# Where a four-layer graph kernel adds up mask quarters, sums squares and takes its spare PSUM banks

## The chip, the cores and the metric

The program runs on one core of a Trainium2 chip. Its metric is the device time of one execution in microseconds (us). Three runs of the kernel before gave 1098.0, 1098.6 and 1100.78 us, so the median is 1098.6 us. The engines are called TensorE (PE in the profile), VectorE (DVE), ScalarE (ACT), GpSimd (POOL) and SyncE (SP).

## The reference

`x` has 8 batches of 2048 nodes with 64 channels. `adj` is a 2048 x 2048 matrix of edges, each row divided by its degree. Four layers follow, each of the form `x = layernorm(x + layer(x))`.

```python
# layer 0: Chebyshev terms of the matrix, weights of each node from its embedding
w = einsum('nd,dkio->nkio', embedding, weight); b = einsum('nd,do->no', embedding, bias)
x_g = [x, A @ x, 2 * A @ (A @ x) - x]
out = einsum('bnki,nkio->bno', x_g, w) + b
# layer 1: attention over entries of adj above 0.5, softmax, elu
# layer 2: ((adj + I) @ (x @ W.T + b)) / degree
# layer 3: v = x with node 0 replaced; three times:
effects = einsum('nm,bmd->bnd', adj, v)
h = relu(concat([v, effects]) @ W1.T + b1); v = h @ W2.T + b2
```

## The kernel before

Nodes lie on the partitions in 16 tiles; the 512 columns are batch times channel, cut into four chunks `c` of 128. A block `(c, j)` is four node tiles of one chunk, 128 partitions x 512 elements; there are 16. The mask (edges as 64 or 0, in fp8) stays in SBUF (`Bm`), and activations are split into a high and a low f16 half, so every product with the mask is two matmuls of 512 columns per tile.

The order of all work is written out by hand in lists that every engine's program walks, each engine picking the steps that it has a part in. `MIDDLE` (`middle_order`, from L94) is layer 0: for each of 64 tiles a step `Z` (36 matmuls against the weights, of which VectorE and ScalarE accumulate the results by the embedding), `add` on GpSimd, and `("bt", 4u + t)`; the norms of layer 0 and most of layer 1 are strewn among them. `TAIL` (`last_order`, from L147) holds layer 2 and the first product of layer 3 as steps `("P", k)`, k = 0 to 31, each a 512-column product over all 16 tiles, with an evacuation `("E", k)`; then the last two products of layer 3, in four halves n = 4 to 7. Each of those is made in Winograd's way by seven instead of eight quarter products: `("M", n, s, q)`, slots s = 0 to 6, for two columns of blocks each. Time there is counted in half slots h = 14 (n - 4) + 2 s + jj, 56 in all; `on(h, ...)` puts a step at the head of a half slot.

What the steps do:

- `bt` (L1581): one of 64 sums of quarters of the mask, 128x512 fp8 (T3, T2, T4, T1, 16 each, in this order; each waits for the one of the array before). The first matmul that needs them is `("M", 4, 2, 0)`, which waits for all 64 (`s_bt`).
- `V` (n, s, jj) (L1486): evacuation of a slot. In slots 1, 4, 5 and 6 a block is finished: `high` writes its high half, one more VectorE instruction the low half (`s_gl`). In slot 6 ScalarE's relu comes first.
- `G`: transform of a finished block by the weights into the input of the next product (PE by `by_weight`, L692; VectorE adds up). `cut` splits it into halves (ScalarE, then GpSimd). `mix`: Winograd's sums of the input, on VectorE.
- `gmax`, `gcol`, `step`: largest value of a half product, sent round the partitions through PE (L924), and a chain of ten small VectorE instructions that makes the next scales. `flags`, `total` (PE, L899), `verdict`: the test whether the input is of the kind that the fast path may take; `branch` stands before h = 28.
- `F` (c, j): last transform of a finished block, four instructions of VectorE add it to `X` (`s_y3`). Then the norm of that block: `sq` (ScalarE squares it into a buffer, VectorE sums groups of 64), `var3` (VectorE, then ScalarE's square root), `rs3` (five small VectorE instructions, L1429 to L1433) and `out` (VectorE multiplies, L1619; SyncE sends 256 KB). The steps F, sq and var3 stand together, rs3 and out one half slot later. 14 blocks go so before the last two (3, 0) and (3, 1).

PSUM has 8 banks. `take_banks` (L528) gives a slot of half product n a fixed pair of them: banks 2 and 3 for slots 1, 3, 5; banks 4 and 5 (n even) or 0 and 1 (n odd) for slots 0, 2, 4, 6. All other steps (`G`, `F`, `t22`, `gcol`, `total`) take turns in the list `banks`: 6, 7 and the two that this half product leaves free. Whoever takes a bank waits for the last reader of what was in it (`held`). Worked out from this, the first matmul of half product 7, `("M", 7, 0, 0)`, waits in bank 0 for `s_y3` = 7, the end of VectorE's part of `("F", 1, 0)`.

Of the kernel before, what the change touches and what calls it, by code (L numbers as in the profile page):

```python
# [93 lines left out]
def middle_order():  # L94
# [30 lines left out]
    for u in range(16):  # L125
# [21 lines left out]
def last_order(after):  # L147
# [34 lines left out]
    at(31, *mixes(4, 1, 1, 3, 2), cut(4, 1, "X12"), cut(4, 1, "S2"), *mixes(4, 1, 4))  # L182
    for k in range(32):
# [30 lines left out]
    on(15, ("total",))  # L214
    on(16, ("verdict",))
    between = {}
    for g in range(2):
        n, h = 6 + g, 14 * (2 + g)
        on(h + 1, ("fin", g))
        for s in ENDS:  # L220
            for jj in range(2):
                u, e = ending(n, s, jj), h + 2 * s + jj
                first, then = [("F", *u), ("sq", 3, *u), ("var3", *u)], [("rs3", *u), ("out", *u)]
                if e == 54:
                    between[55] = first
                    on(56, *then)
                elif e == 55:
                    on(56, *first, *then)
                else:
                    on(e + 2, *first)  # L230
                    on(e + 3, *then)
# [35 lines left out]
def gnn_kernel(nc, x_in, at_in, a_in, embt_in, sm_in, bx_in, w0_in, a12_in, w0bb_in, out):  # L267
    ctx = ExitStack()
    with ctx:
# [733 lines left out]
        def scalar_steps(e, steps):  # L1003
# [3 lines left out]
            for step in steps:  # L1007
# [28 lines left out]
                elif kind == "sq":  # L1036
# [6 lines left out]
                    if SQPREV[L, c, j] is not None:  # L1043
                        e.wait_ge(s_red, SQPREV[L, c, j] + 1)
                    fn(four(sq_buf(L, c, j)), xpart(c, j), ACT.Square).then_inc(s_sq, 1)
                elif kind in ("var", "var3"):
                    L, c, j = (*norm_key(step), 0)[:3]
                    e.wait_ge(s_var, VARN[norm_key(step)] + 1)
                    fn(st_part(L, c, j, 1), st_part(L, c, j, 2), ACT.Sqrt).then_inc(s_sd, 1)
# [255 lines left out]
        def vector_steps(e, steps, fc):  # L1305
# [44 lines left out]
            for step in steps:  # L1350
# [54 lines left out]
                elif kind == "sq":  # L1405
                    L, c, j = step[1:]
                    o = st_part(L, c, j, 0)
                    e.wait_ge(s_sq, SQN[L, c, j] + 1)
                    red(e, o if L == 3 else o[:, 8 * j:8 * j + 8], grid(sq_buf(L, c, j)), ALU.add).then_inc(s_red, 1)
                elif kind == "var":  # L1410
                    L, c = step[1:]
                    e.wait_ge(s_red, SQN[L, c, 3] + 1)
# [6 lines left out]
                elif kind == "var3":  # L1419
                    c, j = step[1:]  # L1420
                    u = order3(c, j)
                    e.wait_ge(s_red, SQN[3, c, j] + 1)
                    e.wait_ge(*((s_n[1], 16) if u < 2 else (s_n[3], u - 1)))
                    ts(e, st_part(3, c, j, 2), st_part(3, c, j, 0), 1 / 64, 1e-5 * 4096, ALU.mult, ALU.add).then_inc(s_var, 1)
                elif kind in ("rs", "rs3"):
                    L, c, j = (*norm_key(step), 0)[:3]
                    e.wait_ge(s_sd, VARN[norm_key(step)] + 1)
                    s0, s1, s2 = (st_part(L, c, j, k) for k in range(3))
# [41 lines left out]
                elif kind == "V" and step[2] not in (0, 2):  # L1470
# [17 lines left out]
                    e.wait_ge(s_gh, place(p, c, j) + 1)  # L1488
                    e.wait_ge(s_gl, place(p, c, j))
# [91 lines left out]
                elif kind == "bt":  # L1581

                    k, q = divmod(step[1], NT)
                    t, cols = q // 2, slice(512 * (q % 2), 512 * (q % 2) + 512)
                    quarters = {f"B{i}{j}": Bm[:, 8 * i - 8 + t, 1024 * j - 1024 + cols.start:1024 * j - 1024 + cols.stop]
                                for i in (1, 2) for j in (1, 2)}
                    d = {f"T{i}": BT[:, i - 1, t, cols] for i in (1, 2, 3, 4)}
                    e.wait_ge(s_bm, 2 * NT)
                    if k:
                        e.wait_ge(s_bt, NT * (k - 1) + q + 1)  # L1590
                    o, a, b, f = ((d["T3"], quarters["B22"], quarters["B12"], ALU.subtract),
                                  (d["T2"], d["T3"], quarters["B11"], ALU.add),
                                  (d["T4"], quarters["B21"], d["T2"], ALU.subtract),
                                  (d["T1"], quarters["B12"], quarters["B11"], ALU.subtract))[k]
                    e.tensor_tensor(o, a, b, f, saturate=False).then_inc(s_bt, 1)
# [600 lines left out]
```

## Time and profile before

| | |
|---|---|
| median of three runs | 1098.6 us |
| profiled execution, its own time | 1096.39 us |
| its span, first to last instruction | 1094.6 us |
| busy: PE, DVE, ACT, POOL | 1032.6, 781.2, 406.6, 456.2 us |
| mean granted TensorE clock | 0.986 |

The profile's rows tell start and length of an instruction in us, the engine, the line in the kernel (often a helper's: L1146 is every scalar_tensor_tensor, L1697 every sum on GpSimd), what it writes and reads, and in square brackets how long the engine had been idle and which instruction ended that. The names are those of the SBUF and PSUM tensors: `BW` is the mask and the sums of its quarters, `S` the split activations, `T` the finished blocks, `X` the running x, `WZ` the weights and later a scratch buffer.

### The profile page before, as it was taken

What the parts mean: (1) busy time and instruction counts of PE and PEld (TensorE: products, weight loads), DVE (VectorE), ACT (ScalarE), POOL (GpSimd) and SP (SyncE); (2) the same over time, 40 slices, a digit from 0 to 9 for tenths busy, and PEclk for the clock granted to TensorE, in tenths of its full rate; (3) what the DMA queues carried; (4) which work ended last, traced back from release to release, by engine and by line L of the source; (5) the groups of instructions that cost most, each with busy time, mean ns of one, the idle gap of its engine ahead of it and who ended that gap; (6) DMA issues with size and microseconds to landing.
All of it is one profiled execution on the core that took longest, in us unless ns stands there. A gap on an engine that the chain in (4) does not pass through costs nothing.

```text
span 1094.6 us, 18614 instructions
## 1 busy us (share of the span) xinstructions
PE 1032.6 (94%) x6922; PEld 494.2 (45%) x6922; DVE 781.2 (71%) x1887; ACT 406.6 (37%) x878; POOL 456.2 (42%) x543
## 2 busy tenths in 40 slices
PE   6989999999999999999999999999999999995993
PEld 2446444434443433334355555555545445552442
DVE  5855676778658876887776877785576867678556
ACT  3632233333334344444424644653445221221211
POOL 0003597546357766885662503443252322222000
PEclk9999999999999999999999999999999999998897
DMA  9750000000000000000010221112112000000111
GB/s 370 258 230 1 1 2 1 1 1 1 1 1 2 1 1 2 1 1 2 1 40 1 78 78 40 66 51 77 65 52 77 1 2 1 3 20 29 30 30 49
DMA packets 14657, 45.65 MB, mean 42 GB/s; under 512 B 960, under 2 KB 9280, under 8 KB 10080
## 3 DMA queue, kind: packets, MB, share of 16 engines
q1 hardware_dynamic: 14560, 44.39, 11.0%
q8 instruction: 57, 0.93, 0.3%
q14 instruction: 40, 0.33, 0.1%
HBM read 40.19 MB, written 4.19 MB: 41 GB/s over the span
## 4 chain that ended last, share of the span: by engine, by line
PE 73%; DVE 14%; POOL 3%; ACT 3%; issue 3%; DMA 2%; SPq 0%; DVEq 0%; ACTq 0%; POOLq 0%
PE PS L713 32%; PE PS L842 17%; PE PS L886 15%; DMA R<-at_in 2%; DVE X L1146 2%; DVE T L1146 2%; PE PS L699 1%; PE PS L700 1%; PE PS L698 1%; POOL X L1697 1%; ACT T L1005 1%; POOL T L1697 1%; DVE R L1146 1%; DVE T L1149 1%; DVE BW L1143 1%
## 5 line engine op out<-in xcount | busy, mean ns | idle before, releaser
L713 PE MATMUL PS<-BW,S 128*128 128x512 fp8e4 x1792 | 405.0, 380 | 8.1 <-DVE R L1146 4.0
L713 PEld LDWEIGHTS PS<-BW,S 128*128 128x128 f16 x1792 | 170.0, 98 | 216.1 <-issue 17.8
L842 PE MATMUL PS<-WZ,R 64*128 64x512 f16 x1536 | 198.9, 377 | 3.2 <-ACT T L1005 3.2
L1005 ACT ACTIVATE T<-PS,SM 128x128 f32<-128x128 f32 x384 | 112.8, 366 | 201.2 <-DVE X L1146 131.0
L1697 POOL TENSOR_TENSOR T<-T 128x128 f32<-128x128 f32 (+1 forms) x192 | 131.0, 682 | 120.5 <-ACT T L1005 109.6
L1146 DVE SCALAR_TENSOR_TENSOR X<-PS,SM,X 128x128 f32<-128x128 f32 x320 | 109.6, 342 | 28.2 <-PE PS L842 27.2
L886 PE MATMUL PS<-BW,S 128*128 128x512 fp8e4 x512 | 117.7, 384 | 10.8 <-DVE X L1146 10.3
L842 PEld LDWEIGHTS PS<-WZ,R 64*128 64x128 f16 x1536 | 69.0, 94 | 107.4 <-issue 25.4
L1697 POOL TENSOR_TENSOR S<-R,S 128x512 f16<-128x512 f32 x48 | 58.1, 1223 | 122.0 <-ACT S L1005 122.0
L842 PE MATMUL PS<-WZ,T 64*128 64x512 f16 x768 | 103.8, 376 | 0.0
L1697 POOL TENSOR_TENSOR T<-R,T 128x512 f16<-128x512 f32 x36 | 42.5, 1181 | 141.2 <-DVE T L1138 80.8
L1146 DVE SCALAR_TENSOR_TENSOR T<-PS,SM,T 128x128 f32<-128x128 f32 x256 | 87.8, 343 | 16.5 <-PE PS L842 16.2
L886 PEld LDWEIGHTS PS<-BW,S 128*128 128x128 f16 x512 | 49.4, 99 | 67.5 <-DVE X L1146 10.5
L1005 ACT ACTIVATE R<-PS,cs 128x512 f32<-128x512 f32 x48 | 32.7, 684 | 112.7 <-PE PS L707 79.0
L886 PE MATMUL PS<-BW,T 128*128 128x512 fp8e4 x320 | 72.8, 379 | 0.0
L698 PE MATMUL PS<-hat,T 128*128 128x128 f16 x320 | 57.2, 220 | 13.4 <-DVE T L1146 13.4
L1697 POOL TENSOR_TENSOR X<-X,T 128x128 f32<-128x128 f32 x128 | 62.6, 489 | 10.0
L765 PE MATMUL PS<-BW,S 128*128 128x512 fp8e4 x240 | 53.8, 386 | 9.3 <-DVE BW L1143 9.3
L842 PEld LDWEIGHTS PS<-WZ,T 64*128 64x128 f16 x768 | 37.4, 94 | 45.5
L700 PE MATMUL PS<-hat,T 128*128 128x128 f16 x320 | 57.2, 220 | 0.0
L699 PE MATMUL PS<-hat,T 128*128 128x128 f16 x320 | 57.2, 220 | 0.0
L1146 DVE SCALAR_TENSOR_TENSOR R<-PS,ra,R 128x128 f32<-128x128 f32 x192 | 52.6, 342 | 6.1 <-PE PS L700 3.5
(214 smaller groups left out, 1434.4 us busy)
## 6 DMA issues: line engine op xcount, KB each, us to landing
WZ<-a_in SPq DMA_DIRECT2D x16, 1024.0 KB, 4.8
R<-at_in SPq DMA_DIRECT2D x15, 1024.0 KB, 6.2
out<-X SPq DMA_DIRECT2D x16, 256.0 KB, 2.3
X<-x_in SPq DMA_DIRECT2D x3, 1024.0 KB, 14.3
T<-w_in SPq DMA_DIRECT2D x1, 1536.0 KB, 9.5
R<-at_in SPq DMA_DIRECT2D x2, 512.0 KB, 4.8
SM<-sm_in SPq DMA_DIRECT2D x1, 520.5 KB, 15.8
X<-x_in SPq DMA_DIRECT2D x2, 256.0 KB, 4.5
```

Of the source, the lines that this page charges most:

```text
L698: e.matmul(ok, th, hat[:, 0, kind, :], start=True, stop=False)
L699: e.matmul(ok, tl, hat[:, 0, kind, :], start=False, stop=False)
L700: m = e.matmul(ok, th, hat[:, 1, kind, :], start=False, stop=True)
L713: m = e.matmul(o, stile(h, t, c), Bm[:, t, block(j)], start=(t == 0 and h == 0), stop=(last and t == NT - 1 and h == 1))
L765: e.matmul(bank(2 * c + j), stile(h, jt, c), Bm[:, jt, block(j)], start=(jt == 0 and h == 0), stop=False)
L842: m = e.matmul(bank(b0 + q), halves[kd][zh][r, :], WZ[r, wh, kd, block(g)], start=(i == 0), stop=(i == 8))
L886: m = e.matmul(o, half_of(n, what, h, q % 2)[:, t, :], b[:, 4 * (q % 2) + t, :], start=(s in (0, 1, 3) and q % 2 == 0 and t == 0 and h == ...
L1005: return e.activation(o, i, f, **kw)
L1143: return e.tensor_scalar(o, i, 0.0, EDGE, ALU.not_equal, ALU.mult, saturate=False)
L1146: return e.scalar_tensor_tensor(out=o, in0=a, scalar=s, in1=b, op0=f, op1=g)
L1149: return e.tensor_reduce(o, i, op=f, axis=AX.X, apply_absolute_value=absolute, negate=negate)
L1697: return e.tensor_tensor(o, a, b, f)
```

## The change

It has these parts.

1. The 64 `bt` steps leave `MIDDLE` and VectorE; they stand in `TAIL` at k = 8 to 29, three to a k, and GpSimd makes them.
2. For n = 5, 6, 7 `gcol` and `step` stand one half slot later, `total` and `verdict` too.
3. From slot 4, second pair, to the end of a half product the other steps take turns in banks 6 and 7 alone.
4. The low half of the blocks of slot 6 is made by GpSimd for n < 7.
5. The norm of layer 3: for the first 14 blocks ScalarE sums the squares itself, in eight activations of 64 columns with an accumulator (`accum_out`) in place of one of 512 columns and VectorE's reduction. `var3` and `rs3` are made for two blocks at once (16 columns in place of 8), and stand later; the two last blocks keep their own. `out` of ten blocks (the first eight and (2, 2), (2, 3)) is made by GpSimd, of the other six by VectorE. `F` and `sq` of the 16 blocks are spread anew.

```diff
-            order += [("Z", u, t), ("add", u, t), ("bt", 4 * u + t)]
+            order += [("Z", u, t), ("add", u, t)]
...
+    for i in range(64):
+        at(8 + i // 3, ("bt", i))
...
-        on(h + 1, ("gcol", p, g), ("step", p, g))
-        on(h + 2, *take(n, 0, "X11"))
+        on(h + 2, ("gcol", p, g), ("step", p, g), *take(n, 0, "X11"))
...
-    on(15, ("total",))
-    on(16, ("verdict",))
+    on(16, ("total",))
+    on(17, ("verdict",))
     between = {}
+
+    for n, s, jj, h in ((6, 1, 0, 33), (6, 1, 1, 34), (6, 4, 0, 41), (6, 4, 1, 42), (6, 5, 0, 43), (6, 5, 1, 44), (6, 6, 0, 44),
+                        (6, 6, 1, 45), (7, 1, 0, 47), (7, 1, 1, 48), (7, 4, 0, 52), (7, 4, 1, 53), (7, 5, 0, 54), (7, 5, 1, 55)):
+        on(h, ("F", *ending(n, s, jj)), ("sq", 3, *ending(n, s, jj)))
+    for n, s, h in ((6, 1, 36), (6, 4, 43), (6, 5, 46), (6, 6, 47), (7, 1, 49), (7, 4, 54), (7, 5, 56)):
+        u = ending(n, s, 0)
+        on(h, ("var3", *u, 2), ("rs3", *u, 2), ("out", *u), ("out", *ending(n, s, 1)))
+    u, v = ending(7, 6, 0), ending(7, 6, 1)
+    between[55] = [("F", *u)]
+    w = half[56]
+    half[56] = [("sq", 3, *u), *w[:2], ("F", *v), ("sq", 3, *v), ("var3", *u, 1), ("rs3", *u, 1), *w[2:], ("out", *u),
+                ("var3", *v, 1), ("rs3", *v, 1), ("out", *v)]
...
+                        elif s == 4 and q == 2:
+                            banks = (6, 7)
...
+        def by_gpsimd(c, j):
+
+            return order3(c, j) < 8 or order3(c, j) in (12, 13)
+
+        def summed_by_act(c, j):
+
+            return order3(c, j) < 14
...
+                        o, q = four(sq_buf(L, c, j)), st_part(L, c, j, 0)
+                        for i in range(8):
+                            t, d = i // 2, slice(64 * (i % 2), 64 * (i % 2) + 64)
+                            m = fn(o[:, t, d], X[:, 4 * j + t, 128 * c + d.start:128 * c + d.stop], ACT.Square, accum_out=q[:, i:i + 1])
+                        m.then_inc(s_sq, 1)
...
+                    if s == 6 and n < 7:
+                        continue
                     e.wait_ge(s_gl, place(p, c, j))
                     stt(e, T[:, c, 1, block(j)], f, 0.0, T[:, c, 0, block(j)], ALU.max, ALU.subtract).then_inc(s_gl, 1)
```

In `gpsimd_steps` the code of `bt` is that of L1583 to L1595, word for word, and three kinds are new:

```diff
+                elif kind == "V" and step[1] < 7 and step[2] == 6:
...
+                    e.wait_ge(s_gh, k + 1)
+                    e.wait_ge(s_gl, k)
+                    add(T[:, c, 1, block(j)], RT[rt_buf(s, jj)], T[:, c, 0, block(j)], ALU.subtract).then_inc(s_gl, 1)
+                elif kind == "out" and by_gpsimd(*step[1:]):
+                    c, j = step[1:]
+                    e.wait_ge(s_rs, RSN[first_of(c, j)] + 1)
+                    e.wait_ge(s_n[3], order3(c, j))
+                    scaled(e, c, j).then_inc(s_n[3], 1)
```

By the same rules of `take_banks`, `("M", 7, 0, 0)` then waits for `s_cp` = 18, ScalarE's copy of `("t22", 6, 1)`, seven half slots earlier.

## Rows read from the trace of the kernel before

**Rows 1.** The page's part 4: the chain that ended last, by engine.
```profile
PE 73%; DVE 14%; POOL 3%; ACT 3%; issue 3%; DMA 2%; SPq 0%; DVEq 0%; ACTq 0%; POOLq 0%
```

**Rows 2.** Windows by stage: length, busy us (instructions) of each engine, clock, DMA share, GB/s.
```profile
113.00:546.00 433.00, 420.62 (x3170) 178.16 (x3172) 320.17 (x893) 166.98 (x478) 282.90 (x388) 1.00 0.00 1
546.00:812.00 266.00, 266.00 (x1776) 142.66 (x1773) 191.67 (x385) 125.59 (x188) 103.61 (x89) 1.00 0.15 56
812.00:990.00 178.00, 174.48 (x1069) 89.31 (x1067) 131.00 (x298) 52.03 (x81) 48.52 (x42) 1.00 0.05 17
990.00:1020.00 30.00, 14.52 (x75) 6.59 (x74) 22.33 (x58) 6.06 (x13) 4.50 (x3) 0.77 0.15 43
...
1072.00:1094.60 22.60, 5.25 (x38) 2.98 (x36) 14.78 (x48) 3.99 (x10) 0.00 (x0) 0.75 0.18 51
```

**Rows 3.** PE's timeline, 995 to 1020 us, and one undisturbed group of 16 at 1061.
```profile
995.18 0.22 PE L698 MATMUL PS<-hat,T 128*128 128x128 f16 x1 [1.78 <-DVE T L1146]
...
1003.49 0.22 PE L698 MATMUL PS<-hat,T 128*128 128x128 f16 x1 [3.38 <-DVE T L1146]
...
1014.64 5.58 PE L886 MATMUL PS<-BW,S 128*128 128x512 fp8e4 x16 [10.32 <-DVE X L1146]
...
1061.18 3.62 PE L886 MATMUL PS<-BW,S 128*128 128x512 fp8e4 x16
```

**Rows 4.** DVE's timeline, 1006 to 1014 us.
```profile
1006.47 1.12 DVE L1146 SCALAR_TENSOR_TENSOR X<-PS,R,X 128x128 f32<-128x128 f32 x4
1008.28 0.69 DVE L1149 TENSOR_REDUCE T<-WZ 128x8 f32<-128x512 f32 x1 [0.69 <-ACT WZ L1005]
...
1013.46 1.12 DVE L1146 SCALAR_TENSOR_TENSOR X<-PS,R,X 128x128 f32<-128x128 f32 x4
```

**Rows 5.** The chain that ended last, pieces in layer 0: start, us, what.
```profile
227.54 0.60 DVE BW L1595
...
273.84 0.60 DVE BW L1595
...
327.50 1.28 POOL X L1697
...
367.33 1.35 DVE BW L1595
```

**Rows 6.** VectorE's sums of mask quarters: ns shortest, median, longest; first and last start.
```profile
L1595 DVE TENSOR_TENSOR BW<-BW x64: 675/682/1701, 125.4 to 549.6; 128x512 fp8e4<-128x512 fp8e4 x64
```

**Rows 7.** Waits of PE, whole span: us, times, longest.
```profile
PE PS L924 <- DVE gmh L1149: 1.9, 2, 1.1
PE PS L899 <- DVE sums L1149: 1.1, 1, 1.1
```

**Rows 8.** GpSimd's groups with two inputs of 512 columns: busy, mean ns, idle before.
```profile
L1697 POOL TENSOR_TENSOR X<-X,bc 128x512 f32<-128x512 f32 x32 | 43.2, 1361 | 10.2 <-DVE S L1146 9.0
L1697 POOL TENSOR_TENSOR T<-R,T 128x512 f16<-128x512 f32 x36 | 42.5, 1181 | 141.2 <-DVE T L1138 80.8 <-ACT T L1005 60.5
```

**Rows 9.** Window of k = 9 to 31, columns as in rows 2.
```profile
618.00:812.00 194.00, 194.00 (x1331) 105.73 (x1330) 142.11 (x285) 96.75 (x141) 70.92 (x58) 1.00 0.18 65
```

**Rows 10.** VectorE's multiplications X by T, 512 columns: ns shortest, median, longest.
```profile
L1439 DVE TENSOR_TENSOR X<-X,T x48: 677/762/1751, 260.3 to 722.6; 128x512 f32<-128x512 f32 x48
```

**Rows 11.** ACT's timeline: a square of 512 columns with its accumulator; three activations of 128.
```profile
31.04 0.61 ACT L935 ACTIVATE T<-X 128x512 f32<-128x512 f32 x1
31.56 0.18 ACT L935 ACTIVATION_READ_ACCUMULATOR T<-X 128x1 f32 x1
31.65 0.61 ACT L935 ACTIVATE S<-X 128x512 f16<-128x512 f32 x1
...
532.92 0.88 ACT L1005 ACTIVATE T<-PS,SM 128x128 f32<-128x128 f32 x3 [0.42 <-DVE T L1146]
```

**Rows 12.** Timeline of the end: PE's wait, and VectorE's last instruction.
```profile
1075.19 0.22 PE L698 MATMUL PS<-hat,T 128*128 128x128 f16 x1 [2.58 <-DVE T L1146]
...
1091.19 0.69 DVE L1619 TENSOR_TENSOR X<-X,T 128x512 f32<-128x512 f32 x1
```

More of the change, by code:

```diff
@@ L213, in last_order @@
     on(14, ("flags",))
-    on(15, ("total",))
-    on(16, ("verdict",))
+    on(16, ("total",))
+    on(17, ("verdict",))
     between = {}
-    for g in range(2):
[L218 to L231, printed above, removed]
+    for n, s, jj, h in ((6, 1, 0, 33), (6, 1, 1, 34), (6, 4, 0, 41), (6, 4, 1, 42), (6, 5, 0, 43), (6, 5, 1, 44), (6, 6, 0, 44),
[9 more added lines that the diff above has]
+                ("var3", *v, 1), ("rs3", *v, 1), ("out", *v)]
+    for g in range(2):
+        on((29, 44)[g], ("fin", g))
     for h in range(57):
@@ L1047, in scalar_steps @@
                     L, c, j = (*norm_key(step), 0)[:3]
+                    m = step[3] if L == 3 else 1
                     e.wait_ge(s_var, VARN[norm_key(step)] + 1)
-                    fn(st_part(L, c, j, 1), st_part(L, c, j, 2), ACT.Sqrt).then_inc(s_sd, 1)
+                    fn(st_part(L, c, j, 1, m), st_part(L, c, j, 2, m), ACT.Sqrt).then_inc(s_sd, 1)
                 elif kind == "row_a":
@@ L1406, in vector_steps @@
                     L, c, j = step[1:]
+                    if L == 3 and summed_by_act(c, j):
+                        continue
                     o = st_part(L, c, j, 0)
@@ L1419, in vector_steps @@
                 elif kind == "var3":
[L1420 to L1424, printed above, removed]
+                    c, j, m = step[1:]
+                    if summed_by_act(c, j):
+                        e.wait_ge(s_sq, SQN[3, c, j + m - 1] + 1)
+                    else:
+                        e.wait_ge(s_red, REDN[3, c, j] + 1)
+                    r = order3(c, j) // 2
+                    e.wait_ge(*((s_n[1], 16) if r < 2 else (s_n[3], 2 * r - 2)))
+                    ts(e, st_part(3, c, j, 2, m), st_part(3, c, j, 0, m), 1 / 64, 1e-5 * 4096, ALU.mult, ALU.add).then_inc(s_var, 1)
                 elif kind in ("rs", "rs3"):
@@ L1427, in vector_steps @@
                     e.wait_ge(s_sd, VARN[norm_key(step)] + 1)
-                    s0, s1, s2 = (st_part(L, c, j, k) for k in range(3))
+                    s0, s1, s2 = (st_part(L, c, j, k, step[3] if L == 3 else 1) for k in range(3))
                     fc(e.reciprocal(s1, s1))
@@ L1580, in vector_steps @@
                     e.wait_ge(s_kg, n)
[L1581 to L1595, printed above, removed]
                 elif kind == "rows":
@@ L1613, in vector_steps @@
                     m.then_inc(s_y3, 1)
-                elif kind == "out":
+                elif kind == "out" and not by_gpsimd(*step[1:]):
                     c, j = step[1:]
-                    e.wait_ge(s_rs, RSN[3, c, j] + 1)
-                    v = xpart(c, j).rearrange("p t (b o) -> p t b o", o=C)
-                    r = st_part(3, c, j, 2).rearrange("p (t b) -> p t b", b=2).unsqueeze(3).broadcast_to([128, 4, 2, C])
-                    e.tensor_tensor(v, v, r, ALU.mult).then_inc(s_n[3], 1)
+                    e.wait_ge(s_rs, RSN[first_of(c, j)] + 1)
+                    e.wait_ge(s_n[3], order3(c, j))
+                    scaled(e, c, j).then_inc(s_n[3], 1)
                 elif kind == "chk":
@@ L1704, in gpsimd_steps @@
                     pool_xs(e, step[1])
+                elif kind == "bt":
+                    k, q = divmod(step[1], NT)
+                    t, cols = q // 2, slice(512 * (q % 2), 512 * (q % 2) + 512)
+                    quarters = {f"B{i}{j}": Bm[:, 8 * i - 8 + t, 1024 * j - 1024 + cols.start:1024 * j - 1024 + cols.stop]
+                                for i in (1, 2) for j in (1, 2)}
+                    d = {f"T{i}": BT[:, i - 1, t, cols] for i in (1, 2, 3, 4)}
+                    e.wait_ge(s_bm, 2 * NT)
+                    if k:
+                        e.wait_ge(s_bt, NT * (k - 1) + q + 1)
+                    o, a, b, f = ((d["T3"], quarters["B22"], quarters["B12"], ALU.subtract),
+                                  (d["T2"], d["T3"], quarters["B11"], ALU.add),
+                                  (d["T4"], quarters["B21"], d["T2"], ALU.subtract),
+                                  (d["T1"], quarters["B12"], quarters["B11"], ALU.subtract))[k]
+                    e.tensor_tensor(o, a, b, f, saturate=False).then_inc(s_bt, 1)
                 elif kind == "add":
@@ L1763, in gpsimd_steps @@
                     add(T[:, c, 1, block(j)], RT[k % 4], T[:, c, 0, block(j)], ALU.subtract).then_inc(s_gl, 1)
+                elif kind == "V" and step[1] < 7 and step[2] == 6:
+                    n, s, jj = step[1:]
+                    k = place(n // 2, *ending(n, s, jj))
+                    c, j = ending(n, s, jj)
+                    e.wait_ge(s_gh, k + 1)
[3 more added lines that the diff above has]
+                    c, j = step[1:]
+                    e.wait_ge(s_rs, RSN[first_of(c, j)] + 1)
+                    e.wait_ge(s_n[3], order3(c, j))
+                    scaled(e, c, j).then_inc(s_n[3], 1)
         BIG = BW[:, :].bitcast(F32)
```

31 lines of the change are left out of this document (24 added, 7 removed).

## The prediction

> **What bounds the kernel now.** I read the chain that ended last first: 73% of it is PE [rows 1]. So the question is only where PE stands still, and the windows by stage tell it, as length less PE's busy time [rows 2]. Layer 0: 433.0 - 420.6 = 12.4 us. Layer 2 and the first product of layer 3: nothing in 266 us. Half products 4 to 6: 178.0 - 174.5 = 3.5 us. The seam from half product 6 to 7: 30.0 - 14.5 = 15.5 us. The end: 22.6 - 5.25 = 17.4 us, most of it after PE's last large group. The rest of the idle time lies before 113 us, where the change has no hand. A saving on DVE, ACT or POOL counts only as far as it shortens one of these.
>
> **Part 1, the mask sums leave VectorE in layer 0.** They take 64 x 0.68 us at the median, with outliers of 1.70 [rows 6], some 53 us of DVE, but PE idled only 12.4 us there. The chain shows how much of that hangs on them. Before 231.7 us (PE waits 2.3 + 0.3) it runs through one sum of 0.60; the rest is the chain of small scale instructions [rows 5]. Before 275 us (wait 1.6) again through one of 0.60 [rows 5]; the rest is VectorE's share of the tile and a reduction. So 0.6 goes at each. Around 361 to 389 us the chain stays on DVE and runs through four sums, the first of 1.35 [rows 5], 4.1 us together, against PE waits of 3.5; I take 2.5, since the last wait keeps its reduction, as at 275. At 340 and 450 us are two more waits of 0.9 each with one or two sums in the chain; I take 1.7 for both. Before 332, 436 and 532 us the chain comes from GpSimd's X of 1.28 us [rows 5] by way of ACT's square, with no mask sum in it: these three waits of 0.95 stay. Gain 0.6 + 0.6 + 2.5 + 1.7 = 5.4 us. Bounds: 2.4 (0.6 at four places) and 9.5 (all but the three).
>
> **The same sums on GpSimd.** The trace has none in fp8 on POOL. With the same shape it has 1.18 us (f16 and f32) and 1.36 us (f32) [rows 8]; below, VectorE's 0.68 [rows 6]. I take 1.2, as the rows nearest in operand widths: 64 x 1.2 = 77 us. From k = 9 to 31 POOL is busy 70.9 of 194 us [rows 9]; with 77 it is at 76%. In its queue the three sums of a k stand behind the D and G halves and ahead of E's low half, which waits for product k anyway; G's halves are made two k (18 us) before PE wants them, and PE has no wait in that stage [rows 2]. So it costs nothing while three sums (3.6 us, at 1.36 4.1) fit in a k of 8.6 us beside POOL's 3.1. If that cover were gone, `("M", 4, 2, 0)` at 831 us would wait.
>
> The Trainium skill speaks against this part: GPSIMD Engine Reference, section 4.1 (Engine selection), gives elementwise work to VectorE and calls GpSimd about 2 times slower for two inputs. The trace agrees on the price (1.18 against 0.68). If it decided here, the part would cost 64 x 0.5 = 32 us; by the trace it decides nothing, as POOL is idle most of that stage.
>
> **Part 2, gcol and total later.** PE waits 1.9 us in two places for gcol's input and 1.1 for total's [rows 7]. Half a slot is 4.1 us of PE work, more than any of these. All go: 3.0 us. What stands behind them on VectorE, G's sums, comes at the same place as before; step's chain delays slot 1's evacuation, of which PE needs the bank two slots later. Bounds 2 and 3.5.
>
> **Parts 3 and 5, the seam at 990 to 1020 us.** PE waits 1.78, 3.38 and 10.32 us, together the 15.5; then 16 matmuls take 5.58 instead of 3.62 us at a granted clock of 0.5 [rows 3], the lower of the two levels, after the engine had stood still: 1.96 more. The 10.32 are the bank: `("M", 7, 0, 0)` waits for F (1, 0) on VectorE, which ended at 1014.6, and DVE works off the norms in order: from one F to the next 7.0 us (1006.47 to 1013.46) [rows 4]. The new bank rule lets M (7, 0, 0) start at once, so none of it is left. The waits of 1.78 and 3.38 are F's transforms waiting for low halves out of the same late queue. By the change VectorE loses a reduction of 0.69 [rows 4] on 14 blocks, half of the rs chains (1.0 each), ten out of 16 multiplications (0.69) and its wait for ACT's square between F and sum. Of the 7.0 us per block about 2.5 stay. Gain 15.5 + 1.96 = 17.4 us; bounds 10 (the two smaller waits and a few us of a new one stay) and 17.4. Part 4 takes 0.69 us from DVE and puts 1.18 [rows 8] on an idle POOL, 0.5 us later; its readers stand slots away: nothing.
>
> **What ACT pays.** A square of 512 columns is followed after 0.52 us by its accumulator read and that by the next after 0.09; activations of 128 follow each other in 0.26 [rows 11]. Eight of at most 0.26 + 0.09 give 2.8 us, with 0.2 for 64 columns 2.4. I take 2.5 instead of 0.52. Worst case, full lengths without overlap: 8 x (0.37 + 0.18) = 4.4. I laid the queues of half product 7 out with 2.5: every V and t22 copy is made at least a half slot before PE asks for it. Behind ACT's sums stand these copies and the square root; behind the root VectorE's rs3, and behind that the next F and V. From 3.1 us a block on, the lag reaches `("F", 3, 2)`.
>
> **The end.** Before: PE waits 2.58 us for V (7, 6, 0) and DVE's last instruction ends at 1091.9 [rows 12], 26.6 us after the last matmul of slot 5. Laid out with the rows' durations the new order brings F (3, 0) at the same place, but then saves an rs chain (1.0) and a reduction (0.7) between PE's last transform and the last block, and two multiplications (0.7 each) go to POOL: the last ends after 23.7 us. Gain 2.9; with ACT sums of 3.7 us it is a loss of 0.4. Bounds -1 and 4. The last transfer stays as it is.
>
> **The sum** against the profiled execution: 1096.4 - 5.4 - 3.0 - 17.4 - 2.9 = 1067.7 us. That execution lies 2.2 us under the median of the three runs; half of that difference I add, since the after runs may lie on either side: 1069.
>
> **The rivals.**
>
> (a) ScalarE becomes the bound. For it: all squares of a block now stand on one queue with the copies that free PE's banks. Against it: ACT is busy 6 us of 30 at the seam [rows 2]. At 3.7 us a block PE waits about 4 us at F (3, 2) and the end loses 3.3: 1069 + 7 = 1076.
>
> (b) VectorE and GpSimd get in each other's way in layer 2. The multiplications X by T take 0.68 us at best and up to 1.75 [rows 10], so a collision costs up to 1.07. The stage has some 37 wide two-input VectorE instructions, at worst 37 x 1.07 = 40 us more on a DVE that is busy 142 of 194 us [rows 9]: 182, just below full, so PE would lose only in bursts, 5 to 10 us: 1077. The Trainium skill, GPSIMD Engine Reference, section 1 (Specifications), names such contention over shared SBUF interfaces for VectorE instructions with two SBUF inputs; that is where it would strike.
>
> (c) Only part of the seam goes. The bank wait is gone, but the transforms F wait for another late low half: half of the 15.5 stays, with the low clock: 1069 + 9 = 1078. For it: the DVE queue still holds all F and V, and rs3 now blocks it while ACT sums.
>
> (d) Slower. GpSimd's fp8 sum is far dearer than its f32 sum. From 611 us (k = 8) to 831 POOL has 220 - 78 = 142 us free, 2.2 us a sum; from there each more tenth delays M (4, 2, 0) by 6.4 us, and from 2.2 + 29 / 64 = 2.65 us on the kernel is slower than before; at 3.0: 1069 + 51 = 1120. Against it: the f16 and f32 forms cost the same within 15% [rows 8], so width hardly counts.
>
> (e) The change doesn't do what it says, as the sums still hold up layer 0's successor or PE's waits in layer 0 stem from elsewhere: only the seam is won, 1069 + 9 = 1078.
>
> **How the numbers follow.** Forecast 0.60; (a) 0.12; (b) 0.10; (c) 0.08; (d) 0.04; (e) 0.03; 0.03 for losses that cancel the gain without any of these. The likeliest: 1069. The known terms' bounds reach from 1096.4 - 9.5 - 3.5 - 17.4 - 4 = 1062 up to 1069 + 3 + 1 + 7 + 4 = 1084; from 1060 (the profiled run's 2 us less) to 1081 it takes in (a), (b), (c) and (e) and leaves out less than 2 in 10. This kernel's measurement tells about 0.3% from no change. Faster by more: 0.93; same 0.03; slower 0.04, by (d).
>
> **What would show it.** Right: no `bt` of DVE before 550 us and 64 of POOL at 1.1 to 1.4 us between 600 and 790; DVE busy some 50 us less in layer 0 and PE idle there 7 us instead of 12.4; no wait of PE over 1 us between 810 and 1060, and a clock of 1.00 there; accumulator reads 14 x 8 more on ACT. Wrong: POOL's sums over 2 us, a new PE wait in the P stage, an M waiting for ACT's T or R in half product 7, or PE waits in layer 0 as before.

## The result and the profile after

The changed kernel takes 1068.6 us (median of 4 runs, 1068.21 to 1068.83), the kernel before in the same runs 1098.4 (1098.0 to 1100.78): a ratio of 0.9724, interval 0.9707 to 0.9741. Measured again beside the last experiments, it was 1067.7 against 1100.8, 0.9698 (0.9679 to 0.9717). The forecast was 1069.0. The profiled execution took 1068.64 us, its span 1066.8.

Windows by stage of the changed kernel, columns as in rows 2:

```profile
113.00:541.00 428.00, 419.30 (x3156) 177.91 (x3155) 275.25 (x832) 164.56 (x473) 273.98 (x389) 1.00 0.01 1
541.00:806.00 265.00, 265.00 (x1783) 142.14 (x1778) 206.63 (x384) 125.37 (x191) 175.57 (x151) 1.00 0.15 53
806.00:980.00 174.00, 173.46 (x1039) 88.20 (x1038) 126.21 (x272) 55.13 (x110) 58.86 (x50) 1.00 0.07 23
980.00:1000.00 20.00, 20.00 (x139) 10.88 (x137) 11.55 (x33) 10.76 (x57) 6.89 (x6) 1.00 0.01 1
1000.00:1050.00 50.00, 48.51 (x288) 24.37 (x285) 28.72 (x81) 19.89 (x137) 6.66 (x7) 1.00 0.16 47
1050.00:1066.80 16.80, 4.03 (x35) 2.37 (x35) 10.13 (x37) 4.48 (x22) 2.08 (x2) 0.76 0.29 83
```

Against [rows 2]: in layer 0 VectorE is busy 45 us less. In the stage after it PE still never stops, though VectorE and GpSimd both do more there. The seam, now at 980 to 1000 us, has no idle time of PE and a full clock.

For every kernel below the span is cut at the same places: "head" runs up to PE's first matmul against the weights (step `Z`), "layer 0" to the last of these, "P" from there to the first matmul of an `M`, "M" to the last one, "end" to the end of the span. All bounds are the starts of these matmuls.

| kernel (profiled execution) | head | layer 0 | P | M | end | span |
|---|---|---|---|---|---|---|
| before | 120.0 | 426.4 | 266.4 | 264.6 | 17.2 | 1094.6 |
| changed | 122.4 | 421.3 | 266.4 | 242.4 | 14.3 | 1066.8 |
| changed, second time | 123.1 | 421.0 | 266.4 | 242.0 | 14.3 | 1066.8 |

So 5.1 us went in layer 0, 22.2 in M, 2.9 in the end, and 2.4 came back in the head, where no code was changed. In all the kernels profiled here but the one before the head takes 121.4 to 123.8 us: the profiled execution of before had an early one. That takes some 2 us off the difference of the two spans, 27.8 us; the medians differ by 29.8 us, and by 33.1 us in the later measurement. Layer 0 is not quite steady either: in the four profiled kernels that make the sums there it takes 426.3, 426.4, 428.2 and 430.1 us, in all the others 421.0 to 421.4.

PE's waits in the changed kernel (us in total, times, longest):

```profile
PE PS L783 <- DVE BW L1175: 7.8, 4, 5.5
PE PS L731 <- DVE T L1178: 5.6, 1, 5.6
PE PS L716 <- DVE T L1178: 3.9, 2, 2.1
PE PS L860 <- ACT T L1023: 3.1, 4, 0.9
```

The first two lie in the head. L716 are the transforms around the last `M` (waits of 1.86 us at 1050.37 and of 2.06 at 1055.63), L860 is layer 0. The 10.32 us wait of [rows 3] and the three waits of [rows 7] have no line any more.

### The profile page after: what moved, and what is told of

The parts are those of the page before. It is cut to its first block, busy times and chain, and to the rows that moved or that the text cites. A ratio compares the mean times of both kernels' runs of the same rounds, so it can differ in the third digit from the quotient of the medians.

```text
span 1066.8 us, 18773 instructions
## 1 busy us (share of the span) xinstructions
PE 1029.9 (97%) x6922; PEld 494.1 (46%) x6922; DVE 726.3 (68%) x1751; ACT 422.6 (40%) x1081; POOL 536.0 (50%) x623
## 4 chain that ended last, share of the span: by engine, by line
PE 82%; DVE 9%; DMA 2%; ACT 2%; POOL 2%; issue 1%; SPq 0%; POOLq 0%; ACTq 0%; DVEq 0%
PE PS L731 33%; PE PS L860 20%; PE PS L904 18%; DMA R<-at_in 2%; PE PS L716 2%; PE PS L718 2%; PE PS L717 2%; DVE T L1178 1%; DVE X L1178 1%; ACT T L1023 1%; PE PS L725 1%; PE PS L723 1%; PE PS L724 1%; DVE BW L1175 1%; DVE S L1178 1%
## 5 line engine op out<-in xcount | busy, mean ns | idle before, releaser
L860 PE MATMUL PS<-WZ,R 64*128 64x512 f16 x1536 | 198.5, 377 | 3.1 <-ACT T L1023 3.1
L1726 POOL TENSOR_TENSOR T<-T 128x128 f32<-128x128 f32 (+1 forms) x192 | 126.6, 660 | 126.1 <-ACT T L1023 115.7
L860 PEld LDWEIGHTS PS<-WZ,R 64*128 64x128 f16 x1536 | 69.3, 94 | 106.7 <-issue 25.4
L860 PE MATMUL PS<-WZ,T 64*128 64x512 f16 x768 | 103.8, 376 | 0.0
L1726 POOL TENSOR_TENSOR T<-R,T 128x512 f16<-128x512 f32 x42 | 49.6, 1187 | 80.5 <-DVE T L1170 55.0
L1748 POOL TENSOR_TENSOR BW<-BW 128x512 fp8e4<-128x512 fp8e4 x64 | 75.4, 1206 | 0.0
L1726 POOL TENSOR_TENSOR X<-X,T 128x128 f32<-128x128 f32 x128 | 59.4, 464 | 10.0
L716 PE MATMUL PS<-hat,T 128*128 128x128 f16 x320 | 56.8, 219 | 3.9 <-DVE T L1178 3.9
L1181 DVE TENSOR_REDUCE T<-T 128x8 f32<-128x512 f32 x32 | 21.9, 686 | 55.8 <-ACT T L1023 55.8
L860 PEld LDWEIGHTS PS<-WZ,T 64*128 64x128 f16 x768 | 37.4, 94 | 45.5
L718 PE MATMUL PS<-hat,T 128*128 128x128 f16 x320 | 56.8, 219 | 0.0
```

The costliest lines, as they stand in the source:

```text
L716: e.matmul(ok, th, hat[:, 0, kind, :], start=True, stop=False)
L718: m = e.matmul(ok, th, hat[:, 1, kind, :], start=False, stop=True)
L860: m = e.matmul(bank(b0 + q), halves[kd][zh][r, :], WZ[r, wh, kd, block(g)], start=(i == 0), stop=(i == 8))
L1181: return e.tensor_reduce(o, i, op=f, axis=AX.X, apply_absolute_value=absolute, negate=negate)
L1726: return e.tensor_tensor(o, a, b, f)
```

## The experiments

Times of a group of kernels were taken on one chip beside the kernel before; each ratio is to that. Two theories of the seam stood against each other. A, the forecast's: the wait of 10.32 us goes by the new bank rule. B: the wait is VectorE's late queue seen through a bank, and the schedule of the norms is enough.

### One part at a time

**The bank rule alone.** In the kernel before:

```diff
                             if m == 4:
                                 held[2] = (s_gt, 14)
+                        elif s == 4 and q == 2:
+                            banks = (6, 7)
```

> The kernel before with part 3 alone: from slot 4, second pair, the other steps take banks 6 and 7. Theory A (the bank is what PE waited for): M (7, 0, 0) no longer waits for VectorE's F (1, 0), the 10.3 us and the low clock's 2.0 go; VectorE's queue is as long as before, so the transform F (1, 1) behind it waits some 3.5 us for the low half of V (6, 6, 1), which VectorE wrote at 1011.2: about 1098.4 - 10.3 - 2.0 + 3.5 = 1090. Theory B (the queue is what PE waited for, and the bank only its last link): the wait moves on to the next transform in full, 1096 to 1098.

Measured: 1093.25 us, ratio 0.9931 (0.9910 to 0.9953), M 257.4 us instead of 264.6. PE's timeline at the seam:

```profile
995.56 3.62 PE L888 MATMUL PS<-BW,S 128*128 128x512 fp8e4 x16
1001.60 0.22 PE L700 MATMUL PS<-hat,T 128*128 128x128 f16 x1 [1.78 <-DVE T L1148]
1002.27 3.62 PE L888 MATMUL PS<-BW,S 128*128 128x512 fp8e4 x16
1009.90 0.26 PE L700 MATMUL PS<-hat,T 128*128 128x128 f16 x1 [3.37 <-DVE T L1148]
...
1011.14 5.81 PE L888 MATMUL PS<-BW,S 128*128 128x512 fp8e4 x16
```

M (7, 0, 0) no longer waits 10.32 us, but the two waits for transforms of [rows 3] stand as they were: the rule takes the one wait and leaves VectorE's queue. It is worth 7.2 us of M by itself, less than A's 8.4: the low clock does not go but comes behind the wait of 3.37 us (16 matmuls in 5.81 us), and two further waits of PE for transforms, of 0.79 and 1.25 us, follow before 1032 us. B's 1096 to 1098, the wait moving on in full, does not come either.

**The schedule of the norms alone**: the blocks' places in the order, ScalarE's sums of the squares, shared square roots, outputs and the low halves of slot 6 on GpSimd; the old bank rule, the sums of the mask on VectorE in layer 0, the column maxima where they were.

```diff
+    for n, s, h in ((6, 1, 36), (6, 4, 43), (6, 5, 46), (6, 6, 47), (7, 1, 49), (7, 4, 54), (7, 5, 56)):
+        u = ending(n, s, 0)
+        on(h, ("var3", *u, 2), ("rs3", *u, 2), ("out", *u), ("out", *ending(n, s, 1)))
...
+                    if L == 3 and summed_by_act(c, j):
```

> The kernel before with parts 4 and 5 alone (low halves of slot 6 on GpSimd, the norm of layer 3 in its new form and order), the old bank rule. Worked out from the code, M (7, 0, 0) then waits for VectorE's F (1, 2), which stands one half slot before it and not right ahead of it. Theory A (the bank rule is needed): the waits of 1.8 and 3.4 us at the seam go and the end gets 3.8 us shorter, the bank wait stays: about 1089. Theory B (VectorE's queue is the cause): the whole seam goes without the bank rule: 1098.4 - 15.5 - 2.0 - 3.8 = about 1077.

Measured: 1078.85 us, ratio 0.9809 (0.9790 to 0.9828), M 246.3 us. Windows at the seam, columns as in rows 2:

```profile
980.00:1000.00 20.00, 20.00 (x122) 10.15 (x120) 14.48 (x31) 5.62 (x23) 7.20 (x6) 1.00 0.01 2
1000.00:1030.00 30.00, 30.00 (x195) 15.78 (x193) 15.99 (x54) 19.26 (x124) 9.96 (x10) 1.00 0.18 53
```

PE stands nowhere and the clock is full, with the old bank rule: the schedule is enough. It does two things at once that no kernel here takes apart. A block costs VectorE less, and F (0, 2), (0, 3) and (1, 0) now stand behind `("M", 7, 0, 0)`, so that by the old rule this M waits for F (1, 2), as the expectation says, and no longer for F (1, 0).

**The mask's sums alone**, moved as in the change:

```diff
-            order += [("Z", u, t), ("add", u, t), ("bt", 4 * u + t)]
+            order += [("Z", u, t), ("add", u, t)]
...
+    for i in range(64):
+        at(8 + i // 3, ("bt", i))
```

> The kernel before with part 1 alone: the 64 mask sums on GpSimd at k = 8 to 29. Theory: layer 0 gets 5 us shorter, as in the changed kernel, nothing else moves: 1093.3. Rival 1 (contention of VectorE and GpSimd in layer 2 costs PE something that the other parts hide): 1096 or more. Rival 2 (the profile before was taken with an early head, and layer 0 gained nothing): 1098.

Measured: 1092.77 us, ratio 0.9932 (0.9911 to 0.9952); layer 0 421.2 us, P 266.4, M 264.4, end 17.3. Of the stages only layer 0 is shorter, by 5.2 us. The medians of this group differ by 7.8; the kernel before was not profiled in it, so the rest has no place in a trace; the three other kernels of the group, with the sums in layer 0, took 426.3 to 430.1 us there.

**The column maxima and the total alone:**

```diff
-        on(h + 1, ("gcol", p, g), ("step", p, g))
-        on(h + 2, *take(n, 0, "X11"))
+        on(h + 2, ("gcol", p, g), ("step", p, g), *take(n, 0, "X11"))
...
-    on(15, ("total",))
-    on(16, ("verdict",))
+    on(16, ("total",))
+    on(17, ("verdict",))
```

> The kernel before with part 2 alone: gcol, step, total and verdict half a slot later. Theory: PE's three waits of 0.9, 1.1 and 1.1 us go, and nothing comes in their place: 1095.3. Rival: the chain of step on VectorE now delays slot evacuations and the seam's queue gets longer, so that what is won is lost at the seam: 1098.

Measured: 1096.72 us, ratio 0.9968 (0.9953 to 0.9982), M 260.9 us: 3.7 less.

Against this group's 1100.55 the four take 7.3, 21.7, 7.8 and 3.8 us, together 40.6; the whole change takes 33.1. The three without the bank rule make 33.3. Each of these times is known to within some 2 us. So the bank rule should be worth next to nothing once the norms are rescheduled; the next kernel asks that directly.

**The changed kernel without the bank rule:**

```diff
-                        elif s == 4 and q == 2:
-                            banks = (6, 7)
```

> The changed kernel without its part 3 alone: the first M of slot 7 goes back to the pair of banks whose readers end half a slot later. The forecast had put the 10.32 us wait of the seam down to that rule, so by it (theory A) the time is about 1079 and the trace shows one wait of PE of about 10 us near 990 to 1000. By the theory of the queue (B), which the kernel with part 5 alone has already spoken for at 1078.85, VectorE's order of work made the reader late, and that order is the new one here: no wait of PE over 1 us between 980 and 1030, and the time of the changed kernel, 1068.6 within 1.5.

Measured: 1068.58 us (1067.63 to 1069.66), ratio 0.9698 (0.9684 to 0.9711), the ratio that the changed kernel had when it was measured again; M 242.0 us. It goes by theory B: the rule is worth nothing here, to within some 2 us. Its windows of the seam, then VectorE's part of F (1, 2) and `("M", 7, 0, 0)`, which waits for it by the old rule:

```profile
980.00:1000.00 20.00, 20.00 (x133) 10.67 (x132) 11.60 (x31) 10.28 (x57) 6.19 (x5) 1.00 0.01 1
1000.00:1030.00 30.00, 30.00 (x175) 14.95 (x173) 16.46 (x52) 13.64 (x88) 7.36 (x7) 1.00 0.25 71
```

```profile
988.05 1.12 DVE L1176 SCALAR_TENSOR_TENSOR X<-PS,R,X 128x128 f32<-128x128 f32 x4
```

```profile
991.50 3.62 PE L902 MATMUL PS<-BW,S 128*128 128x512 fp8e4 x16
```

The reader is done at 989.2 us, 2.3 before the M starts.

### The engine or the place: the sums on VectorE beside layer 2

```diff
+                elif kind == "bt":
...
+                    o, a, b, f = ((d["T3"], quarters["B22"], quarters["B12"], ALU.subtract),
+                                  (d["T2"], d["T3"], quarters["B11"], ALU.add),
+                                  (d["T4"], quarters["B21"], d["T2"], ALU.subtract),
+                                  (d["T1"], quarters["B12"], quarters["B11"], ALU.subtract))[k]
+                    e.tensor_tensor(o, a, b, f, saturate=False).then_inc(s_bt, 1)
```

These lines go from GpSimd's queue to VectorE's, at the same places of the order.

> The 64 sums of the mask's quarters stay beside layer 2, as in the changed kernel, but VectorE makes them and not GpSimd. If it was the place in time that paid and not the engine, the time is that of the changed kernel, 1068.6 within 1.5: VectorE is busy about 192 us of the 266 before the first M in the kernel before, and 64 sums of 0.68 us are 43 us more, 235 of 266, which still leaves 31. If the engine was needed, VectorE's own work for PE (the transforms and the adds of the blocks) comes later by up to some 2 us at each place where two or three sums stand in one step, and PE waits in pieces between 600 and 810: 1075 to 1090.

Measured: 1075.36 us (1074.29 to 1075.6), ratio 0.9760 (0.9745 to 0.9775). The place pays in full (layer 0 421.3 us), but P is 272.7 us, 6.3 longer. First VectorE's timeline before the wait, then PE's at it, then the window around it:

```profile
746.87 1.28 DVE L1178 SCALAR_TENSOR_TENSOR T<-PS,T 128x512 f16<-128x512 f32 x2
748.06 3.45 DVE L1640 TENSOR_TENSOR BW<-BW 128x512 fp8e4<-128x512 fp8e4 x3
...
753.68 2.28 DVE L1181 TENSOR_REDUCE ra<-WZ 128x1 f32<-128x2048 f32 x1
755.87 0.15 DVE L1181 TENSOR_REDUCE gmh<-gm 128x1 f16<-128x8 f16 x1
```

```profile
756.17 0.22 PE L942 MATMUL PS<-i,gmh 128*128 128x128 f16 x1 [3.91 <-DVE gmh L1181]
```

```profile
750.00:770.00 20.00, 16.09 (x104) 8.39 (x102) 19.51 (x46) 5.25 (x7) 8.78 (x9) 0.91 0.15 59
```

One instruction of 0.15 us, the maxima that `gcol` sends through PE, comes at the end of a queue that is busy 19.5 of 20 us. PE loses 3.9 us for it and, at a granted clock of 0.91 in that window, about 2 more. A group of 32 matmuls right behind the wait takes 8.75 us where later ones take 7.07. Nowhere else in P does PE wait over 0.2 us. GpSimd is thus worth 6 to 7 us here, though a sum takes it 1.2 us and VectorE 0.68. That holds for these places in the order: no kernel here gives the sums other places on VectorE, away from that one instruction. The Trainium skill, GPSIMD Engine Reference, section 4.1 (Engine selection), would leave the sums with VectorE; the measurement decides against it for this stage.

### How much an engine's slower work would have cost

**ScalarE's squares twice.** Each block's eight squares and sums are made twice, nothing else changed:

```diff
+                        for i in range(8):
+                            t, d = i // 2, slice(64 * (i % 2), 64 * (i % 2) + 64)
+                            m = fn(o[:, t, d], X[:, 4 * j + t, 128 * c + d.start:128 * c + d.stop], ACT.Square, accum_out=q[:, i:i + 1])
+                        m.then_inc(s_xx, 1)
```

> The changed kernel, but ScalarE squares and sums each of its blocks of the seam and the end twice, so that a block takes it about 3.9 us and not the 1.92 us of its trace. By the prediction's rival (a): from 3.1 us a block on the lag reaches F (3, 2) and at 3.7 us PE waits about 4 us there and the end loses 3.3, so 1068.6 + 7 = 1076, 1079 at 3.9. If ScalarE's lag is taken up by the order of the queues, there is no new wait of PE between 980 and 1030, and only the end is later by the two or three blocks behind the last matmul: 1070 to 1073.

Measured: 1081.64 us, ratio 0.9818 (0.9794 to 0.9843), 14.0 over the changed kernel. M is 254.8 us, the end 14.7. A block's sixteen squares and sums take ScalarE 4.0 us (from 1020.66 to 1024.64). PE's timeline:

```profile
1029.91 1.89 PE L906 MATMUL PS<-BW,R 128*128 128x512 fp8e4 x8
1038.15 0.26 PE L718 MATMUL PS<-hat,T 128*128 128x128 f16 x1 [6.35 <-DVE T L1186]
...
1039.39 5.82 PE L906 MATMUL PS<-BW,S 128*128 128x512 fp8e4 x16
1046.36 3.62 PE L906 MATMUL PS<-BW,S 128*128 128x512 fp8e4 x16
...
1061.70 0.27 PE L718 MATMUL PS<-hat,T 128*128 128x128 f16 x1 [3.91 <-DVE T L1186]
...
1068.60 0.22 PE L718 MATMUL PS<-hat,T 128*128 128x128 f16 x1 [2.45 <-DVE T L1186]
```

The first wait is that of F (3, 2), behind slot 4 and ahead of slot 5 of half product 7, the place that rival (a) named. At its 3.7 us a block it put 4 us there; at 4.0 it is 6.35, and 16 matmuls take 5.82 us for 3.62 behind it. So ScalarE does become the bound, and the forecast's order holds because a block takes 1.92 us.

**The sums on GpSimd twice and three times.**

```diff
+                    pc(e.tensor_tensor(o, a, b, f, saturate=False))
                     e.tensor_tensor(o, a, b, f, saturate=False).then_inc(s_bt, 1)
```

> The changed kernel, but GpSimd makes each of the 64 sums of the mask's quarters twice, about 2.4 us a sum instead of 1.2. By the prediction's rival (d): GpSimd has room for 2.2 us a sum and each tenth above delays M (4, 2, 0) by 6.4 us, so 0.2 above it is 13 us: 1081. If GpSimd's own work beside layer 2 can be delayed further than was reckoned, or less of it stands there, M (4, 2, 0) waits less: 1068.6 to 1072. The working of PE beside it should show whether VectorE's two-input operations grow: 0.86 us a copy of S in the kernel before and 1.32 in the changed kernel, where GpSimd is busy 176 of 265 us; with 240 of 265 busy, 1.5.

> The changed kernel, but GpSimd makes each of the 64 sums of the mask's quarters three times, about 3.6 us a sum. By the prediction's rival (d): 1.4 us above the point of 2.2, by 64 is 90 us late, so M (4, 2, 0) starts 90 us later: 1158, slower than the kernel before. The break-even that was put at 2.65 us a sum is checked by the slope between this kernel and the one with two: 64 x 1.2 = 77 us between them if GpSimd is the bound in both.

Measured: 1095.8 us, ratio 0.9956 (0.9937 to 0.9976), with 153.1 us of sums, 2.39 a step; and 1164.09 us, ratio 1.0573 (1.0554 to 1.0593), with 222.3 us, 3.47 a step. P is 290.7 and 360.3 us, 24.3 and 93.9 longer than 266.4. Between the two kernels P grows 69.6 us for 69.2 us of work: GpSimd is the bound in both. Where the line meets no loss is then 2.39 - 24.3 / 64 = 2.01 and 3.47 - 93.9 / 64 = 2.00 us a sum, not 2.2. With each sum made twice, a window of P and then PE's waits there:

```profile
600.00:800.00 200.00, 189.97 (x1280) 102.52 (x1278) 167.91 (x269) 93.11 (x137) 190.65 (x161) 0.97 0.16 59
```

```profile
743.74 0.27 PE L706 MATMUL PS<-dg,S 128*128 128x128 f16 x1 [5.17 <-DVE S L1178]
...
833.82 8.90 PE L904 MATMUL PS<-BW,S 128*128 128x512 fp8e4 x32 [9.14 <-DVE R L1178]
```

GpSimd is busy 190.7 of 200 us, and 4.8 of the other 9.3 are waits, nearly all for ScalarE. The delay comes out earlier than forecast: not at M (4, 2, 0), which reads the sums, but from 661 us on at the work that stands behind them in the queue, which VectorE waits for and then PE. Ahead of the first M (833.8 us) it is 9.1 us. With three copies GpSimd's S holds up P's own products, and GpSimd has no wait left in the window:

```profile
PE PS L731 <- POOL S L1726: 56.7, 7, 10.1
```

```profile
600.00:880.00 280.00, 222.21 (x1406) 115.34 (x1404) 173.14 (x283) 101.12 (x147) 270.35 (x232) 0.88 0.13 46
```

### A shorter end

```diff
-    for n, s, h in ((6, 1, 36), (6, 4, 43), (6, 5, 46), (6, 6, 47), (7, 1, 49), (7, 4, 54), (7, 5, 56)):
+    for n, s, h in ((6, 1, 36), (6, 4, 43), (6, 5, 46), (6, 6, 47), (7, 1, 49), (7, 5, 56)):
...
-    between[55] = [("F", *u)]
-    w = half[56]
-    half[56] = [("sq", 3, *u), *w[:2], ("F", *v), ("sq", 3, *v), ("var3", *u, 1), ("rs3", *u, 1), *w[2:], ("out", *u),
-                ("var3", *v, 1), ("rs3", *v, 1), ("out", *v)]
+    w, z = half[56], ending(7, 4, 0)
+    between[55] = [("F", *u), *w[:2]]
+    k = half[54].index(("sq", 3, *ending(7, 5, 0)))
+    half[54][k:k + 1] = [("var3", *z, 2), half[54][k], ("rs3", *z, 2), ("out", *z), ("out", *ending(7, 4, 1))]
+    half[56] = [("sq", 3, *u), ("F", *v), ("sq", 3, *v), *w[2:], ("var3", *u, 2), ("rs3", *u, 2), ("out", *u), ("out", *v)]
```

> The changed kernel with a shorter end: the variance and the scaling of the pair before the last M are put ahead of it, the next pair's variance stands ahead of the squares of the last pair's first block, and the last two blocks share one variance, one square root and the two outputs after it. In the trace of the changed kernel VectorE's last work ends 22.8 us after the last matmul of slot 5 and PE has waits of 1.86 and 2.06 us near 1050 and 1055. If these waits are the queue's (VectorE busy with the variance that stands ahead of a reader of PE's banks), 4 us go: 1064.5. If the end is bound by the matmuls and the one chain behind the last of them, nothing goes that lies ahead of the last matmul and only the one shared variance does: 1067.5 to 1068.6.

Measured: 1065.32 us (1062.86 to 1065.56), ratio 0.9667 (0.9654 to 0.9681), against 0.9698 (0.9684 to 0.9711) on the same chip for the changed kernel without the bank rule: 3.3 us less. It is the fastest of all. M is 240.3 us and the end 13.6: the last M starts at 1048.08 instead of 1051.04 us (0.9 of that is a shorter head), as the wait of 1.86 before it is gone, and one wait of 3.25 at 1053.87 has taken the place of the 2.06. The queue's part of the expectation holds for the larger share of the gain; 0.7 of the expected 4 us is not there.

## Why the forecast was right, step by step

**The sum.** Against the profiled execution it said 1067.7 us, and 1068.64 was measured. Part of this closeness is luck, as two deviations cancel: the head, 2.4 us longer in code that the change does not touch, and terms that were 1.5 us too small together (5.1 + 22.2 + 2.9 = 30.2 for 5.4 + 3.0 + 17.4 + 2.9 = 28.7). Two of the signs that the forecast named did not come: PE is idle 8.7 us in layer 0, not 7, and it has waits over 1 us before 1060, those of 1.86 and 2.06 us at 1050.37 and 1055.63.

**Layer 0**: 5.4 forecast, 5.1 measured, 5.2 with that part alone. Cutting out of each stretch of the chain only the sums in it was a good measure; the 45 us of VectorE's work were not. PE's idle time fell by 3.7 us, from 12.4 to 8.7, where the forecast had it fall to 7, and the rest of the gain lies in its busy time (420.6 to 419.3 us), whose records differ by about as much between two executions. In the four kernels with layer 0 as before this stage took 426.3 to 430.1 us and without the sums 421.0 to 421.4, so that the gain lies between 5 and 9 us by the execution that is taken, and the forecast's 5.4 is near its lower end.

**The sums on GpSimd**: 1.2 us forecast, and no loss in P. The group of GpSimd that decides it, from the changed kernel:

```profile
L1748 POOL TENSOR_TENSOR BW<-BW 128x512 fp8e4<-128x512 fp8e4 x64 | 75.4, 1206 | 0.0
```

P is 266.4 us in both kernels. The reckoning of GpSimd's room in rival (d) was off: 2.2 us a sum, measured 2.0. Two of its assumptions failed. The sums were thought to be late only at their reader, but what stands behind them in the queue was late first. And the queue was reckoned as full to the last microsecond, but with three copies GpSimd is busy 270.4 of 280 us without a wait: by this 3.4% some 0.12 of the 0.2 us, an estimate; the rest was not traced. The break-even moves from 2.65 to 2.0 + 29 / 64 = 2.45, and the kernel with 2.39 us a sum, still 5.0 us faster than before, puts it at 2.39 + 5.0 / 64 = 2.47. There was still 0.8 us of room a sum.

**Rival (b)**, contention, came true in kind, at less than half of its worst size, and not in effect. VectorE's groups from 600 to 800 us, of the kernel before, the changed one, the one with the sums on VectorE, and the one with each sum made twice on GpSimd:

```profile
L1146 DVE SCALAR_TENSOR_TENSOR R<-PS,ra,R 128x128 f32<-128x128 f32 x88 | 23.7, 342 | 0.0
L1146 DVE SCALAR_TENSOR_TENSOR S<-X,cs,S 128x384 f16<-128x384 f32 x4 | 2.4, 608 | 0.0
```

```profile
L1178 DVE SCALAR_TENSOR_TENSOR R<-PS,ra,R 128x128 f32<-128x128 f32 x88 | 23.7, 343 | 0.0
L1178 DVE SCALAR_TENSOR_TENSOR S<-X,cs,S 128x384 f16<-128x384 f32 x4 | 5.0, 1238 | 0.0
```

```profile
L1178 DVE SCALAR_TENSOR_TENSOR S<-X,cs,S 128x384 f16<-128x384 f32 x4 | 2.4, 607 | 0.0
```

```profile
L1178 DVE SCALAR_TENSOR_TENSOR S<-X,cs,S 128x384 f16<-128x384 f32 x4 | 6.0, 1496 | 0.0
```

The same instruction takes 0.61 us where GpSimd is busy 73 or 71 of these 200 us, 1.24 where it is busy 147 and 1.50 at 191, while the one that reads a bank of PE's and one operand elsewhere stays at 0.34. Over all 16 copies of S, those of 512 columns too, the mean goes from 0.86 us to 1.32 and, with each sum made twice, to 1.47, where 1.5 was expected. In all it costs VectorE 15 us of P (191.7 to 206.6 busy, [rows 2]), where rival (b) had up to 40; VectorE stays at 78% and PE loses nothing. The Trainium skill, GPSIMD Engine Reference, section 1 (Specifications), names this contention for instructions with two inputs in SBUF; these rows agree.

**Part 2**: 3.0 forecast, 3.7 measured alone. The three waits are gone; the 0.7 us beyond them was not traced.

**The seam**: 17.4 forecast. M lost 22.2 us, less 3.7 of part 2, which leaves 18.5, and 18.3 with the norms alone. Of that 0.7 is the wait before the last M (2.58 us before, 1.86 now), which the forecast counted to the end; 17.8 stay. The size was right. The cause was wrong in one step: "The new bank rule lets M (7, 0, 0) start at once, so none of it is left". With the rule undone that M starts as early (991.50 us, with a head 1.4 us later, to 990.50). F (1, 0), the reader that held the bank, was late because VectorE worked off seven-microsecond blocks. In the new order the F follow each other in 3.5 to 4.3 us there, and F (1, 0) stands behind the M: the old rule's reader is F (1, 2), done in time. Which of the two, the cheaper blocks or the later places, would have been enough alone was not run. The rule by itself takes 7.2 us from the kernel with the old schedule and nothing from the one with the new. The forecast gave the rule the largest wait of its sum, 10.32 us; that the sum still came out is luck, since the schedule stood in the same change and took that wait too.

**ScalarE's share**: 2.5 us a block forecast, 1.92 measured. ScalarE's timeline of one block in the changed kernel (first, second and last square, and the copy behind it):

```profile
988.20 0.26 ACT L1023 ACTIVATE WZ<-X 128x64 f32<-128x64 f32 x1 [1.74 <-DVE X L1178]
988.36 0.19 ACT L1023 ACTIVATION_READ_ACCUMULATOR WZ<-X 128x1 f32 x1
988.45 0.24 ACT L1023 ACTIVATE WZ<-X 128x64 f32<-128x64 f32 x1
...
989.88 0.24 ACT L1023 ACTIVATE WZ<-X 128x64 f32<-128x64 f32 x1
990.03 0.18 ACT L1023 ACTIVATION_READ_ACCUMULATOR WZ<-X 128x1 f32 x1
990.12 0.67 ACT L1023 ACTIVATE R<-PS,cs 128x512 f32<-128x512 f32 x1
```

The eight come 0.24 us apart. Rival (a) stays a rival with its place confirmed: at 4.0 us a block it would have cost 14 us.

**The end**: 2.9 forecast and 2.9 measured, but not from the same mark, so that the match is luck. The stage "end" starts at the last M; the forecast reckoned from slot 5. The last group of slot 5 starts at 1061.18 us before [rows 3] and at 1037.08 now:

```profile
1037.08 3.62 PE L904 MATMUL PS<-BW,S 128*128 128x512 fp8e4 x16
```

```profile
1063.44 0.69 DVE L1191 TENSOR_TENSOR X<-X,T 128x512 f32<-128x512 f32 x1
```

From there to the end of VectorE's last instruction it was 30.70 us [rows 12] and is 27.05, a gain of 3.65; the 0.7 more is the shorter wait before the last M.

**Rivals (c), (d), (e)** did not come: no wait is left at the seam, a sum takes GpSimd 1.2 us, and layer 0 gives its share.

## What to carry to other kernels

A wait for a buffer names the reader that was late, and need not be the fault of the rule that assigned the buffer: before changing the assignment ask why the reader was late, since an assignment that pays alone can be worth nothing beside the reordered queue, as here. Work that no engine needs soon can go to the slower engine if that one is idle in that stage; what counts there is the room in its queue (here 2.0 us a sum for sums of 1.2) and what stands behind it, not only its own reader. Measure gains of parts together as well as apart: here the four parts alone add to 40.6 us and the whole gives 33.

## What the runs showed of the hardware

- A square of 64 columns with its sum costs ScalarE 0.24 us from one start to the next, as the 0.18 us read of the accumulator overlaps the end of its square and the start of the next; eight of them are 1.92 us, and twice as many, with a pause of 0.2 between the halves, 4.0 us.
- GpSimd's two-input sum in fp8 over 512 columns takes 1.10 us at the median (mean 1.21), about the 1.18 of f16 [rows 8]; VectorE's takes 0.68 [rows 6].
- A VectorE instruction with two operands outside PE's banks grew from 0.61 to 1.24 and 1.50 us as GpSimd's sums came beside it, once and twice (means of four, GpSimd busy 73, 147 and 191 of 200 us).
- GpSimd with its queue full and no wait in the trace was busy 270.4 of 280 us (each sum made three times).
- After a wait of 6.35 us, 16 matmuls took 5.82 us, and after one of 10.32 us 5.58 [rows 3], against 3.62; after one of 3.37, in the kernel with the bank rule alone, 5.81. The low clock added about 2 us to each of these stops of PE.
